# Attention with a mixture of experts: the preparation of keys and of query tiles at other slots

## The reference

```
xn = layernorm(x)                         # no weights
s  = attention(xn, norm_g, Wq, Wkv, Wout, out_norm_g)
g  = silu(ffn(xn, wr, w1, b1, w2, b2))
x  = x + s * g

attention: xn2 = layernorm(xn) * norm_g
           q = xn2 @ Wq      (8 heads of 64);   k, v = xn2 @ Wkv   (one head, shared)
           q, k = 4 * l2norm(q), 4 * l2norm(k)
           out = softmax(q k^T) v, all heads side by side, @ Wout, then layernorm * out_norm_g
ffn:       logits = xn @ wr.T; the best 2 of 8 experts for each row, softmax of the two
           every expert takes at most 2560 rows: gelu(x @ w1 + b1) @ w2 + b2, weighted and added up
```

## Time and profile before

| | us |
|---|---|
| median of three runs | 2855.59 |
| the profiled execution's own time | 2853.52 |
| its span in the profile | 2851.8 |
| TensorE busy | 2726.3 |
| VectorE busy | 2044.2 |
| ScalarE busy | 1902.4 |
| GpSimd busy | 643.2 |

### The profile page before, as it was taken

One profiled execution on the slowest core, in us unless ns is written; L12 is line 12 of the kernel. 1 busy time (PEld: TensorE's weight loads), 2 busy tenths in 40 slices (PEclk: granted clock), 3 DMA queues, 4 the chain that ended last, 5 costly groups with the idle time before them and its releaser, 6 DMA issues.

```text
span 2851.8 us, 86213 instructions
## 1 busy us (share of the span) xinstructions
PE 2726.3 (96%) x38213; PEld 1822.8 (64%) x38277; DVE 2044.2 (72%) x3077; ACT 1902.4 (67%) x2435; POOL 643.2 (23%) x428
## 2 busy tenths in 40 slices
PE   4999999998999989999999999999999999999996
PEld 3666666655666656676677667676666666666664
DVE  5888888889888853433433333338999999999986
ACT  6777767766677665655655655547777777777763
POOL 3111111113888100000000000002344343434312
PEclk8999999999999999999999999999999999999997
DMA  3223222102433011212212212101112121111101
GB/s 104 92 75 118 76 87 96 43 28 68 140 130 113 17 33 58 76 53 83 77 53 69 91 53 69 55 28 38 33 54 60 47 59 48 54 44 53 43 21 44
DMA packets 111013, 184.12 MB, mean 65 GB/s; under 512 B 12648, under 2 KB 78128, under 8 KB 110640
## 3 DMA queue, kind: packets, MB, share of 16 engines
q1 hardware_dynamic: 98352, 145.04, 15.5%
q0 software_dynamic: 12288, 33.57, 3.8%
HBM read 92.58 MB, written 85.98 MB: 63 GB/s over the span
## 4 chain that ended last, share of the span: by engine, by line
PE 85%; ACT 5%; DVE 5%; issue 3%; DMA 1%; POOL 1%; SPq 0%; POOLq 0%; DVEq 0%; ACTq 0%
PE pair L603 24%; PE bank L682 15%; PE pair L668 14%; PE bank L624 8%; PE bank L632 7%; PE bank L622 7%; PE bank L584 3%; PE bank L542 2%; ACT arena L838 2%; DVE arena L1193 2%; PE bank L652 1%; PE bank L554 1%; PE bank L572 1%; PE bank L511 1%; ACT oT L718 0%
## 5 line engine op out<-in xcount | busy, mean ns | idle before, releaser
L1193 DVE TENSOR_TENSOR arena<-arena 128x1024 bf16<-128x1024 f32 (+1 forms) x1032 | 1219.9, 1212 | 162.7 <-ACT arena L838 160.6
L838 ACT ACTIVATE arena<-pair 128x1024 f32<-128x1024 f32 (+1 forms) x1032 | 1017.6, 1017 | 326.9 <-PE pair L603 321.2
L603 PE MATMUL pair<-qT,kT 128*128 128x512 f16 (+1 forms) x4096 | 879.2, 383 | 37.7 <-ACT arena L838 34.8
L622 PE MATMUL bank<-vhl,arena 128*128 128x65 bf16 x8192 | 647.2, 193 | 4.7 <-DVE att L1186 4.7
L624 PE MATMUL bank<-vhl,arena 128*128 128x64 bf16 x8192 | 648.3, 195 | 0.0
L622 PEld LDWEIGHTS bank<-vhl,arena 128*128 128x128 bf16 x8192 | 566.7, 99 | 56.2 <-DVE att L1186 5.0
L624 PEld LDWEIGHTS bank<-vhl,arena 128*128 128x128 bf16 x8192 | 548.5, 97 | 51.6 <-issue 0.8
L603 PEld LDWEIGHTS pair<-qT,kT 128*128 128x128 f16 (+1 forms) x4096 | 199.6, 95 | 484.7 <-issue 413.5
L1242 POOL TENSOR_TENSOR q_small<-q_small,minus_half 128x8 f32<-128x8 f32 x64 | 146.2, 2284 | 1352.2 <-DVE q_small L1106 1352.0
L854 ACT ACTIVATE h_f<-pair,b1T 128x512 f32<-128x512 f32 x320 | 219.4, 686 | 333.6 <-PE pair L668 333.6
L682 PE MATMUL bank<-w_hl,arena 128*128 128x256 bf16 x3840 | 425.7, 273 | 0.6 <-DVE att L1209 0.6
(11 more groups left out here) (190 smaller groups left out, 2072.9 us busy)
## 6 DMA issues: line engine op xcount, KB each, us to landing
routed_rows<-h_f SPq DMA_DIRECT2D x80, 256.0 KB, 4.7
att<-routed_rows SPq DMA_DIRECT2D x40, 512.0 KB, 4.3
expert_rows<-att SPq DMA_DIRECT2D x40, 512.0 KB, 2.9
raw<-in_L_ffn_w SPq DMA_DIRECT2D x32, 512.0 KB, 4.1
xn_rows<-s_hl SPq DMA_DIRECT2D x16, 512.0 KB, 2.9
xT_out<-xn_rows SPq DMA_DIRECT2D x64, 128.0 KB
w_lo<-in_L_attn_x SPq DMA_DIRECT2D x64, 128.0 KB
out<-w_lo SPq DMA_DIRECT2D x64, 128.0 KB
```

Source lines behind the costliest of these rows:

```text
L603: t = nc.tensor.matmul(into, kT[g // BG % 2][rows, part, keys], qT[g % 2][rows, h, :], start=(turn == 0), stop=(turn == 1))
L622: nc.tensor.matmul(bank[:, at:at + DH + 1], p_top[:, s, cols, 1], V[:, kb, 0:DH + 1], start=(kb == 0 and qb == 0), stop=False, skip_group_ ...
L838: nc.scalar.activation(p_f32[:, n % NP, columns(n)], pairs[n % 2][:, columns(n)], ACT.Exp).then_inc(exped, 1)
L1193: nc.vector.tensor_tensor(p_lo[:, n % NP, c], p_f32[:, n % NP, c], p_top[:, n % NP, c, 1], ALU.subtract).then_inc(lowed, 1)
```

## The change

Five numbers that place side work change. `KV_AT` of groups 4 to 15 goes from slot 38 to slot 36, `K_TURN` for them from 12 to 8 slots, so their keys are transposed at slot 44 where it was slot 50. For query tiles 4 to 63 the scaling on VectorE goes from 4 to 5 slots behind `Q_AT`, the high half on ScalarE from 6 to 7, and the low half on VectorE from 8 to 9. The transpose stays at 11. No instruction is added or removed.

```
--- before.py
+++ after.py
@@ -163,8 +163,8 @@
     S_SHIFT, S_NORM, S_HI, S_LO, S_TURN, S_HALF, S_LOGITS = [
         [early] * BG + [late] * (NG - BG) for early, late in ((3, 5), (4, 7), (5, 9), (6, 11), (9, 14), (1, 2), (3, 4))]
     KV_AT = [12 + 6 * g for g in range(BG)]
-    KV_AT += [base[g - BG] + 38 for g in range(BG, NG)]
-    K_TURN = [9] * BG + [12] * (NG - BG)
+    KV_AT += [base[g - BG] + 36 for g in range(BG, NG)]
+    K_TURN = [9] * BG + [8] * (NG - BG)
     Q_AT = [12 + 6 * j for j in range(GT)]
     for t in range(GT, NT):
         Q_AT.append(base[t // GT - 1] + 16 * (t % GT))
@@ -798,7 +798,7 @@
                 act.wait_ge(q_lo, t_id)
                 nc.scalar.activation(q_n[:, :, :].rearrange("p h n -> p (h n)"), bank, ACT.Square,
                                      scale=rstd[:, g, 1, j:j + 1]).then_inc(q_squared, 1)
-                yield from clock.at(Q_AT[t_id] + 6)
+                yield from clock.at(Q_AT[t_id] + (6 if t_id < GT else 7))
                 act.wait_ge(q_scaled, t_id + 1)
                 act.wait_ge(q_turned, t_id)
                 cast(q_his, q_n[:, :, :].rearrange("p (a b) n -> p a b n", b=2)).then_inc(q_hi, 1)
@@ -1105,12 +1105,12 @@
                 dve.wait_ge(q_sum, t_id + 1)
                 nc.vector.tensor_scalar(q_small[:, 1, :], q_small[:, 0, :], SCALE ** 2 / (SCALE ** 3),
                                         MIN_NORM ** 2 / SCALE ** 3, ALU.mult, ALU.max).then_inc(q_var, 1)
-                yield from clock.at(Q_AT[t_id] + (5 if t_id < GT else 4))
+                yield from clock.at(Q_AT[t_id] + 5)
                 dve.wait_ge(q_rstd, t_id + 1)
                 nc.vector.tensor_tensor(q_n[:, :, :], q_f[:, :, :],
                                         q_small[:, 2, :].unsqueeze(2).to_broadcast([P, H, DH]),
                                         ALU.mult).then_inc(q_scaled, 1)
-                yield from clock.at(Q_AT[t_id] + (7 if t_id < GT else 8))
+                yield from clock.at(Q_AT[t_id] + (7 if t_id < GT else 9))
                 dve.wait_ge(q_hi, t_id + 1)
                 nc.vector.tensor_tensor(q_los, q_n[:, :, :].rearrange("p (a b) n -> p a b n", b=2), q_his,
                                         ALU.subtract).then_inc(q_lo, 1)
```

## The result

The changed kernel takes 2897.63 us, the median of 4 runs (2894.68 to 2901.12), against 2854.56 (4 runs) before: a ratio of 1.0151, 95% interval 1.0134 to 1.0169, some 43 us slower. The forecast was 2885; the range with 8 chances in 10 was 2861 to 2899, the forecast's own 2877 to 2897. The direction is right and the time lies in the wide range, 1.4 us under its upper end, and just above the narrow one; of the 43 us the forecast had 31.6, so the size was too small by a quarter. The profiled execution took 2899.08 us, its span 2897.3.

A forecast was written before the change was run, and what follows sets the result against it. TensorE was taken to bound the kernel; 9.4 us (keys' place), 13.7 (other query tiles) and 8.5 (clock) made 31.6 on 2853.5, so 2885 us; own range 2877 to 2897, 8 in 10 range 2861 to 2899.

The forecast's parts named there:

- What bounds the kernel: Whole kernel: TensorE sets the time, busy 2726.3 of 2851.8 us; the change can only remove or make waits.
- The transpose's wait at the keys' place: Seventh group, slot 43: the query tile's transpose waits 2.47 us for its low half, starting 1.86 us later than today.
- The term of the keys' place: Twelve groups where keys are prepared: gains and new waits sum to +9.4 us, before the clock's 8.5.
- only change places: Ahead of slot 42, seventh group: the copies' pair and the plain pair swap order, keeping the 0.61 us saved.
- The fifth group: Routing group: turning the keys at slot 44 avoids a 2.87 us wait behind a routing result: -2 us.
- The other query tiles: The 48 tiles not at the keys' place: later low halves make transposes wait, +13.7 us, bounds 0 and 15.9.
- The clock: Sixth to twelfth group: new waits make TensorE's clock fall five times of seven, 8.5 us, bounds 0 and 12.
- the second: Rival: VectorE absorbs the one-slot moves and only the keys' place costs, 2863 us; chance 0.1.
- the third: Rival: at slot 43 the query's low half is ready, so all is gain, 2842 us; chance 0.07.
- The first: Rival: same waits in attention but TensorE's clock stays up, 2877 us; chance 0.2.

The follow-up runs named there:

- the keys alone: Kernel before with only the keys moved, KV_AT at 36 and K_TURN 8, queries staying at 4, 6 and 8: 2849.55 us, ratio 0.9983.
- the high half alone: Kernel before with only the query's high half on ScalarE moved to slot 7: 2850.72 us, ratio 0.9985.
- the queries alone: Kernel before with only the three query edits (scaling 5, high half 7, low half 9), keys at 38 and 50: 2871.85 us, ratio 1.0062.

## Why the prediction was right, and where its size was off

- What bounds the kernel: right. TensorE's waits make up 35 of the 45 us, its slower clock most of the rest.
- The transpose's wait at the keys' place: right in kind, 2.47 us forecast, 2.05 to 2.11 measured as idle time in the sixth and the eighth to eleventh group. Counted as the forecast counts, by the start of the transpose within its pair, it is 2.21: the eighth group's pair takes 5.64 us (1007.88 to 1013.53, where it took 3.43). Two errors work against each other in it: TensorE comes to slot 42 0.52 us later than reckoned, because of the bank, and the low half is ready 0.26 us later. In the twelfth group the wait is 2.77: there three instructions of `combine` (1.39 us, L1156 to L1168) stand in the stretch that VectorE works through ahead of the low half. In the seventh it is 3.10, 0.94 of it for GpSimd (I had not followed the change to GpSimd): the keys' power, L1242, stands in its queue behind two scatter DMAs of 2.08 and 1.89 us. GpSimd in the changed kernel (start, duration, engine, line, operation):

```profile
888.25 2.08 POOL L1270 DMA_INDIRECT routed_rows<-xT_out,scatter_to  x1 [0.20 <-issue]
890.63 1.89 POOL L1270 DMA_INDIRECT routed_rows<-xT_out,scatter_to  x1 [0.30 <-issue]
892.55 1.73 POOL L1242 TENSOR_TENSOR k_small<-k_small,minus_half 128x4 f32<-128x4 f32 x1
```
- The term of the keys' place was mis-sized: 9.4 us of waits and 8.5 of clock forecast, 17.9; between slots 36 and 51 of the twelve groups TensorE loses 30.5 us more than before. The step that failed most is the sentence that let the pair of the copies and the plain pair ahead of it "only change places". At slot 36 the projection of keys follows the output projection of slot 35 in the same bank, and must wait until VectorE has written `s_rows` from it (L1143), work that at slot 38 was long done. In a plain group this is 0.25 us of wait and 0.44 of time:

```profile
861.31 0.29 PE L511 MATMUL bank<-wkv_hi,xT 128*128 128x128 bf16 x2 [0.25 <-DVE s_rows L1143]
```

  (this row is of the kernel with the keys alone). Where VectorE has normalisation or routing beside it, it is up to 4.9 us of time a pair; over all groups the pair of slot 36 loses 12 us more than before. That this is close to the missing 12.6 is partly chance. In a plain group a late TensorE only waits less at the transpose: the eighth loses 2.12 us where 1.86 were forecast. What is missing lies in the second, fourth, fifth and sixth group, where the bank costs 1.4 to 4.9 us, and in the third and twelfth, where the transpose stalls longer than reckoned (4.28 and 2.77 us). The keys alone lose the same 12 us at slot 36, and over slots 36 to 51 they come out 4.4 us better than before: the pairs of slots 40, 42, 48 and 50 give it back. The changed kernel gets the same back at slots 40, 48 and 50. Of the 34.9 us between the two, 29.8 lie in the pair of slot 42, where the transpose stalls, and 5.0 in that of slot 44, where the clock falls.
- The fifth group: forecast -2, measured +0.6 in these slots. The turn of the keys did get out of the routing's way, but the projection at slot 36 waits 3.2 us there.
- The other query tiles: 13.7 us forecast, 14.3 measured. In the groups behind the experts the waits are about as read off: for the last tile but one the same working gives 1.14 and 1.14 was measured, for the last 0.95 and 0.77. In the first groups five waits are 1.46 us where I had 0.75, for normalisation's small instructions (L924 to L933) stand ahead of the low half within the slot; and outside slots 36 to 51 the sixth group came out 5 us better than before, where I had let relief of 1.5 us meet its new waits. The errors about cancelled, so that this term fits so well is luck.

```profile
114.99 0.61 PE L554 MATMUL bank<-ident,qhl 128*128 128x128 f16 x8 [1.46 <-DVE qhl L1115]
...
2713.36 0.61 PE L554 MATMUL bank<-ident,qhl 128*128 128x128 f16 x8 [1.14 <-DVE qhl L1115]
...
2741.90 0.61 PE L554 MATMUL bank<-ident,qhl 128*128 128x128 f16 x8 [0.77 <-DVE qhl L1115]
```

- The clock: five falls of seven forecast, four came (sixth, seventh, ninth and twelfth group), at waits of 2.06, 3.10, 2.11 and 2.77 us; three waits of 2.05 to 2.07 had none. Five of seven was a guess, and that it nearly held says little: with the high half alone the third group has the wait of 1.85 us of the earlier trace rows again, and the clock stays up (1.00 over the 5 us in which it was 0.66 before):

```profile
387.00:392.00 5.00, 3.17 (x46) 2.00 (x47) 3.54 (x3) 5.00 (x7) 0.00 (x0) 1.00 0.00 2
```

  Within attention the clock is at half for 34 us in all, against 20 before, which is 7 us of full speed; 8.5 was forecast. The Trainium skill, "TensorE: Matmul & The Clock Gate", section "HAM oscillation — how this bites in real kernels", has it that gaps of this length leave the clock up; the traces say that they sometimes do and sometimes don't.
- The rivals: the second (only the keys' place costs) is refuted by the queries alone, the third (faster) by the first line of the waits. The first, that the clock stays up, is refuted by the windows.

## What to carry to other kernels

Where an order is written out by hand, moving a writer one slot later costs what the slack between it and its reader does not cover: read how much earlier the writer ends than the reader starts, place by place, and add whatever stands ahead of the writer within its new slot. A move that gains alone (3 us here) can cost much beside another (19 us alone, 43 together) when the two bring their work into the same slot of one engine, so look at the order of the built program. And follow a moved step in every resource that it takes, here a PSUM bank that the step before had not yet given back.

## What was not expected of the hardware

On the two other chips the kernel before takes 2889 and 2892 us against 2853. Profiles from there lose their time in the sixth and seventh attention group, where rows are scattered. TensorE stops between the matmuls of `weigh` for nothing that the profile shows. Idle times of the lines L632 and L622 that end with "issue", in the kernel with the keys at 36 and the high half at 7, and the window around one such place against about the same slots of the keys alone, on the chip with 2853:

```profile
PE bank L632 <- issue: 7.7, 17, 1.1
PE bank L622 <- issue: 5.5, 12, 1.1
```

```profile
832.00:842.00 10.00, 6.04 (x78) 3.68 (x75) 3.14 (x3) 2.92 (x4) 6.95 (x7) 0.76 0.40 133
```

```profile
813.00:823.00 10.00, 10.00 (x195) 6.75 (x192) 9.10 (x11) 7.16 (x9) 7.87 (x8) 1.00 0.45 146
```

One pair of slots takes 9.46 us there where it takes 3.43 on the chip of the keys alone, with about the same DMA traffic (133 and 146 GB/s). What holds the instructions up was not tried.
